# Two roundings of a feed-forward stage: constants formed on ScalarE, and a pair's rounding sum put behind the next pair's scaling

## The reference, cut to what matters

```python
def fp4_quant_dequant(x):            # BLOCK = 16 along the last dimension
    scale = jnp.maximum(jnp.max(jnp.abs(xb), axis=-1, keepdims=True) / 6.0, 1e-12)
    idx = jnp.searchsorted(_MID, jnp.abs(xb / scale))
    return (_GRID[idx] * jnp.sign(xb / scale) * scale).reshape(shape)
...
gate = fp4_linear(x, w_gate)
y = fp4_linear(x, w_up)
h = jax.nn.silu(gate) * y
return fp4_linear(h, w_down)         # both operands of fp4_linear are quantised
...
x = x + 0.5 * _L0_ffn_ref(_layernorm(x, axis=-1), L0_ffn_w_gate, L0_ffn_w_up, L0_ffn_w_down)
```

## Time and profile before

| | us |
|---|---|
| runs of the kernel, median of 3 | 1034.25 (1032.65 to 1035.71) |
| the profiled execution, its own time | 1042.43 |
| its span, first to last instruction | 1040.7 |
| FP4 stage one: first h (L307) to last residual (L315) | 40.94 to 107.09 |
| FP4 stage two: the same | 435.18 to 500.63 |

### The profile page before, as it was taken

How to read it: one execution, slowest core, us unless ns; L and a number is a source line. 1 busy time by engine, 2 the same in 40 slices (tenths; PEclk the granted TensorE clock), 3 DMA queues, 4 the chain that set the end, 5 groups by cost and what they waited for, 6 DMA issues and landing times. The chain is left out here.

```text
span 1040.7 us, 15374 instructions
## 1 busy us (share of the span) xinstructions
PE 739.7 (71%) x5487; PEld 502.4 (48%) x5487; DVE 710.3 (68%) x1213; ACT 346.7 (33%) x591; POOL 414.6 (40%) x597
## 2 busy tenths in 40 slices
PE   0566897777779995476577925488887778467694
PEld 0345455776679984254544613233333333254462
DVE  8997778999958885998342337678887786054132
ACT  0211381110015500122112514066766666411152
POOL 4344304888859601344151532223223332115053
PEclk9987899999969998688587967589999999868797
DMA  8000000000000003100012126484000000001213
GB/s 190 10 1 1 1 1 1 1 1 1 1 1 2 1 1 92 45 1 0 1 37 71 41 76 203 107 125 68 9 7 9 8 8 8 7 0 34 70 37 106
DMA packets 43024, 35.98 MB, mean 35 GB/s; under 512 B 6182, under 2 KB 37478, under 8 KB 42950
## 3 DMA queue, kind: packets, MB, share of 16 engines
q1 hardware_dynamic: 40390, 29.68, 12.2%
q0 software_dynamic: 2560, 5.31, 1.5%
HBM read 17.51 MB, written 15.89 MB: 32 GB/s over the span
## 5 line engine op out<-in xcount | busy, mean ns | idle before, releaser
L1990 DVE TENSOR_REDUCE blockmax<-c_bank 128x8 f32<-128x1024 f32 x144 | 174.9, 1223 | 47.5 <-PE c_bank L2116 41.3
L2053 ACT ACTIVATE PT<-c_bank 128x1024 f32<-128x1024 f32 x144 | 145.4, 1025 | 71.4 <-PE c_bank L2138 71.3
L2152 PE MATMUL c_bank<-PT,V 128*9 128x256 f32 (+3 forms) x960 | 78.6, 431 | 14.5 <-POOL PT L1942 10.4
L897 PE MATMUL sums<-prod,ident 128*128 128x128 f32 x512 | 68.2, 290 | 26.6 <-DVE prod L929 26.6
L2109 PE MATMUL c_bank<-KA,QA 48*128 48x128 bf16 (+3 forms) x608 | 59.9, 282 | 36.1 <-DMA KA<-qk_parts_dram 16.3
L1942 POOL TENSOR_SCALAR_AFFINE_SELECT PT<-PT 128x256 f32<-128x256 f32 x128 | 49.0, 406 | 80.8 <-ACT PT L2053 80.8
L897 PEld LDWEIGHTS sums<-prod,ident 128*128 128x128 f32 x512 | 62.7, 200 | 31.9 <-DVE prod L929 31.7
L1648 POOL DMA_INDIRECT routed_results<-results_m,rows_m x48 | 45.9, 957 | 78.0 <-DVE results_m L1625 74.9
L2138 PE MATMUL c_bank<-QA,KA 51*128 51x128 bf16 (+3 forms) x480 | 56.9, 302 | 16.7 <-DMA QA<-nrows 16.1
L1631 DVE TENSOR_TENSOR r_h_m<-r_silu_m,r_gu_m 128x256 f32<-128x256 f32 x48 | 20.2, 421 | 67.1 <-ACT r_silu_m L1616 67.1
L379 PE MATMUL gu_f<-gu_wT,xqT_f 128*128 128x352 f32 x128 | 52.9, 568 | 16.9 <-DVE h_f L307 16.9
(11 more groups left out here) (337 smaller groups left out, 1818.6 us busy)
## 6 DMA issues: line engine op xcount, KB each, us to landing
sorted_rows<-blank SPq DMA_DIRECT2D x2, 1584.0 KB, 12.2
rows_m<-sorted_rows SPq DMA_DIRECT2D x12, 264.0 KB, 4.4
qk_parts_dram<-qk_parts SPq DMA_DIRECT2D x8, 384.0 KB, 3.4
QA<-qk_parts_dram SPq DMA_DIRECT2D x6, 384.0 KB, 7.4
KA<-qk_parts_dram SPq DMA_DIRECT2D x6, 384.0 KB, 9.2
back_m<-routed_results SPq DMA_DIRECT2D x8, 256.0 KB, 3.8
qk_parts_dram<-qk_parts SPq DMA_DIRECT2D x8, 256.0 KB, 3.4
m_gu<-in_rt_gate SPq DMA_DIRECT2D x1, 1024.0 KB, 5.6
```

Of the source, the lines that this page charges most:

```text
L897: ins = nc.tensor.matmul(sums[:, kind, 0], k.ident[:, :], prod[:, kind, e // HALF, :, e % HALF, :], start=(e == 0), stop=(e == DH - 1))
L1990: nc.vector.tensor_reduce(blockmax[:, h % 2, :, HALFQ * n:HALFQ * (n + 1)], slot_of((1, m)).rearrange("p b (n c) -> p b n c", c=P), AX.X, ...
L2053: nc.scalar.activation(PT[:, u % PRING, :, :], slot_of((0, u)), ACT.Exp, scale=SCALE).then_inc(s_pt, 1)
L2152: ins = nc.tensor.matmul(O[32 * g:32 * g + DH + 1, f * P:f * P + n], V[:, b, j, h, :], PT[:, u % PRING, b, o:o + n], start=(j == 0), stop= ...
```

## The change

Only the quantising of h changes, in both FP4 stages. ACT forms the magic number in two operations on the 128 x 704 tile, Relu(p - 1) and then 1.5 x 2^22 x (p' + 1) as one multiply and add, in place of DVE's one operation L173; bias operands are two new columns, `less` and `more`, filled by DVE at the stage's start. Scaled values go to a new tile `hs` with two slots. On DVE the rounding sum of pair j (now `round_h(j)`) is put behind `quantise_h(j+1)`, which holds the first six steps of the next pair. The condition `wait(dve, s_hq, j - 1)` in `quantise_h(j)` is left as it is.

```diff
+    def on_vector_scaled(self, ch, src, slot, xs, s_power):
...
+        ch.link(nc.vector.tensor_tensor(self.blocks(xs), self.blocks(src), self.spread(self.inv[:, :]), ALU.mult))
+        nc.vector.tensor_scalar(magic.bitcast(I32), xs.bitcast(I32), EXPONENT_BITS, None, ALU.bitwise_and).then_inc(s_power, 1)
+
+    def on_scalar_above(self, slot, less):
+        magic = self.magic[:, slot, :]
+        return self.nc.scalar.activation(magic, magic, ACT.Relu, bias=less)
+
+    def on_scalar_magic(self, slot, more):
+        magic = self.magic[:, slot, :]
+        return self.nc.scalar.activation(magic, magic, ACT.Identity, bias=more, scale=GRID_MAGIC)
+
+    def on_vector_sum(self, slot, xs):
+        return self.nc.vector.scalar_tensor_tensor(self.y[:, slot, :], xs, ONE_BELOW, self.magic[:, slot, :], ALU.mult, ALU.add)
...
+        hs = k.sb(f"hs{tag}", [P, 2, W2], ctx=ctx)
+        less = k.sb(f"less{tag}", [P, 1], ctx=ctx)
+        more = k.sb(f"more{tag}", [P, 1], ctx=ctx)
...
-                    qh.on_vector(chh, h[:, :, :].rearrange("p s c -> p (s c)"), j % 2, s_hy)
+                    qh.on_vector_scaled(chh, h[:, :, :].rearrange("p s c -> p (s c)"), j % 2, hs[:, j % 2, :], s_power)
+
+                def round_h(j):
+                    dve.wait_ge(s_magic, j + 1)
+                    qh.on_vector_sum(j % 2, hs[:, j % 2, :]).then_inc(s_hy, 1)
...
+                quantise_h(0)
                 for j in range(PAIRS):
-                    quantise_h(j)
+                    if j + 1 < PAIRS:
+                        quantise_h(j + 1)
+                    round_h(j)
...
+                def magic(j):
+                    act.wait_ge(s_power, j + 1)
+                    qh.on_scalar_above(j % 2, less[:, 0:1]).then_inc(s_above, 1)
+                    act.wait_ge(s_above, j + 1)
+                    qh.on_scalar_magic(j % 2, more[:, 0:1]).then_inc(s_magic, 1)
...
+                magic(0)
                 for j in range(PAIRS):
                     if j + 2 < PAIRS:
                         gate(j + 2)
+                    if j + 1 < PAIRS:
+                        magic(j + 1)
                     hidden_columns(j)
```

More of the change, by code:

```diff
@@ L161, in spread @@
         return ap.unsqueeze(2).to_broadcast([P, self.nb, QBLOCK])
-    STEPS = 7
+    def on_vector_scaled(self, ch, src, slot, xs, s_power):
+        nc, magic = self.nc, self.magic[:, slot, :]
+        ch.link(nc.vector.tensor_reduce(self.amax[:, :], self.blocks(src), AX.X, ALU.max, apply_absolute_value=True))
+        ch.link(nc.vector.tensor_scalar(self.scale[:, slot, :], self.amax[:, :], 1.0 / 6.0, 1e-12, ALU.mult, ALU.max))
+        ch.link(nc.vector.reciprocal(self.inv[:, :], self.scale[:, slot, :]))
+        ch.link(nc.vector.tensor_tensor(self.blocks(xs), self.blocks(src), self.spread(self.inv[:, :]), ALU.mult))
[8 more added lines that the diff above has]
+        return self.nc.vector.scalar_tensor_tensor(self.y[:, slot, :], xs, ONE_BELOW, self.magic[:, slot, :], ALU.mult, ALU.add)
     def on_vector(self, ch, src, slot, s_y):
@@ L276, in fp4_ffn @@
         qh = Quant(k, f"h{tag}", W2, ctx)
+        hs = k.sb(f"hs{tag}", [P, 2, W2], ctx=ctx)
+        less = k.sb(f"less{tag}", [P, 1], ctx=ctx)
+        more = k.sb(f"more{tag}", [P, 1], ctx=ctx)
+        s_const, s_power, s_above, s_magic = (k.sem(f"{n}{tag}") for n in ("s_const", "s_power", "s_above", "s_magic"))
         gu = k.ps(f"gu{tag}", [P, 2, 2, BANK], ctx=ctx)
@@ L315, in residual @@
                     nc.vector.scalar_tensor_tensor(xs, y[:, j % 2, 0:2 * D], 0.5, xs, ALU.mult, ALU.add).then_inc(s_res, 1)
+                nc.vector.memset(less[:, :], -1.0)
+                nc.vector.memset(more[:, :], GRID_MAGIC).then_inc(s_const, 1)
                 if prepare:
@@ L440, in _ @@
                 gate(1)
+                act.wait_ge(s_const, 1)
+                magic(0)
                 for j in range(PAIRS):
```

## The result

| | us |
|---|---|
| the kernel before, median of 6 runs | 1034.98 (1032.65 to 1038.26) |
| the changed kernel, median of 6 | 1050.86 (1046.85 to 1055.53) |
| ratio of the runs, 95% interval | 1.0151 (1.0114 to 1.0189) |
| profiled execution, own time and span, before | 1042.43, 1040.7 |
| the same, changed | 1051.57, 1049.8 |

What follows compares the result with a forecast made beforehand. DVE set the pace before, at 6.70 us a pair; afterwards two loops would, with a swinging clock, at 8.83. Each stage grows 10.6 us, two stages 21.3, so 1034.25 + 21.3 = 1055.5 us; range 1043 to 1067.

Steps and rivals of the forecast that it cites:

- The gain of L173: DVE time freed by removing L173: 0.56 us per pair, 9.0 us for sixteen, if DVE stayed the bound.
- Loop A: FP4 stages, DVE and POOL: L168 waits for POOL's work behind the rounding sum; period 7.23 us.
- loop B: FP4 stages, all engines, two pairs long through PE's in-order work: 14.71 us, 7.36 per pair; limit at high clock.
- Loop C: One-pair loop through PE and ACT with both new operations; the prediction gave it only at low clock, 11.04 us.
- The start of a stage: First sums of a stage: last input quarter until 64.5, sum of pair 2 ending at 70.0 in stage one.
- The operations on ACT: Relu and Identity on ACT: 0.85 us each, hidden by 0.14 us at the high clock.
- The clock: PE's clock swings, four tenths of the steady part low: 8.83 us per pair, between ends of 7.36 and 11.04.
- the 2.88: PE idle time in us, before the change, behind which slow operations stood; taken as a gap that lost the clock.
- the formula 4P - 24.7: Lengthening of one stage, P being the steady period per pair: 10.6 us at 8.83; two stages 21.3 us.
- The end of a stage: POOL does pairs 6 and 7 back to back, 6.5 us; from POOL's last end to the residual nothing changes.
- the first rival: PE's clock stays high in both stages: 7.36 us per pair, +9.4, 1043.7 us; chance 0.20.
- The idle time of DVE: Profile sign: DVE idle about 2.1 us a pair, ahead of h for silu and of L168 for POOL's hq.

Runs made afterwards that it cites:

- the edit that cut B: Changed kernel with gate_up and silu taken one pair further ahead on PE and ACT; 1050.37 us, ratio 1.0101.
- both edits: Changed kernel with a third slot for POOL's scale and magic, and gate_up and silu one pair further ahead; 1038.25 us, ratio 0.9998.
- filler: Changed kernel with three unused products on the identity put on PE ahead of the transposes for pairs 2 to 5; 1048.53 us, ratio 1.0137.
- the order without ACT: Changed kernel with L173 put back on DVE and no magic number work on ACT; 1063.73 us, ratio 1.0230.

## Why the prediction was right

*The bound before and the loops.* Right. The gain of L173 never came, since DVE stopped being the bound. Taking either loop away alone changed the two stages by less than 3 us; taking both away gave a period of 6.02 against the 6.14 worked out for a DVE-bound kernel. Loop A measured 7.19 for 7.23, loop B 7.34 for 7.36. Loop C was named at the low clock only. Its terms in the prediction come to 7.21 at the high clock, as long as A, and every second period measured 7.24; the edit that cut B cut C with it, so they were not told apart.

*The start of a stage.* Right to 0.4 us in stage one, and there in part by luck. Sum(0) ends at 51.81 (51.83 in the sum), L168(2) starts at 55.13 (55.08), sum(1) ends at 58.99 (59.06), the quarter at 64.40 (64.5), sum(2) at 69.68 (70.0). L169 of pair 3 stood 0.60, so it took 0.4 of the 0.6 that I had added. But the 6.00 us from h(0) to h(1) that I carried over came from a gate_up(1) mostly at the low clock, 4.15 us in the trace of before, and by chance 4.30 in that of the changed kernel. In stage two it took 2.60, and sum(2) ended 27.1 us after the first h and not 28.8 as in stage one. Counting stage one twice put 2 us too much into the start of the second.

*The operations on ACT.* 0.87 and 0.88 for 0.85. I had them hidden by 0.14 us. Measured, they are hidden by less than 0.1 in one ordinary period and tie with the transposes in the next. Where gate_up was slow they stood on the path: the copies at 97.44 start 2.55 us after their transposes, where 0.91 is enough. In stage two, where another gate_up follows, the next silu still came 7.24 us later, so nothing of the lost time was made up. The Trainium skill, page "ScalarE: Activation LUTs", section "Rules for kernel authors", gives add, mul and relu to VectorE because it is faster per element, by up to about three times in bf16. The tiles here are fp32, and in this case that choice would have been the slower one: with the operation on DVE the two stages are 11.2 us longer in the changed order and 7.4 longer with both edits, since DVE's 0.56 us lie on the path. The estimate of 0.89 us by that page's budget agrees with the measured 0.87 and 0.88.

*The clock: the term that was mis-sized.* I took four tenths of the steady part at the low clock, P = 8.83. Measured is (100.66 - 69.68)/4 = 7.75 in stage one and (496.48 - 465.66)/4 = 7.71 in stage two. Against my ends of 7.36 and 11.04 that is one tenth. Three periods in four kept the high clock through gaps of 1.45 to 1.64 us ahead of the transposes and 0.94 behind them; one in each stage lost it, behind a gap of 1.63 in stage one and of 1.45 in stage two, so the length of the gap alone does not say which. That period cost 1.6 to 1.7 us and not 3.7, since only part of it was slow. The rows of before had not told on which side a gap of 1.6 us would fall, and I had placed it too near to the 2.88. The 2.88 was itself read too strongly: the slow product at 97.01 in the earlier trace rows stands behind 0.94 us, and in stage two of before the transposes behind such a gap, at 488.08, took 0.88 us, so that the clock fell only behind them. With the measured P, 7.75 and 7.71, the formula 4P - 24.7 gives 6.3 and 6.1 us, measured 6.7 and 5.7. That the sums agree, 12.4 us, is in part luck, since errors in the start and in the end of the stages partly cancel.

*The end of a stage.* 6.5 us in the sum, 107.53 - 100.66 = 6.87 measured. Sum(7) ran beside POOL, took 1.44 and not 0.88, and held POOL's next operation up, 1.91 for 1.39. I had priced the two in a row without their meeting on the port; it is 0.4 us a stage. From POOL's last end to the residual I had said that nothing changes. It is 6.23 us for 5.93, but by other steps: the transposes start 2.13 us after POOL's end, behind PE's product of pair 6, where before they waited for POOL alone, and the last transposes and product gain 1.8 by a higher clock. In the kernels where that clock stayed low the same stretch takes 7.95 us. So here two errors of about 2 us cancelled.

*The rivals.* In the stages the first rival, the clock staying high, was the nearer one: 9.4 us against my 21.3, with 12.4 measured. In the whole time my 1055.5 is nearer to the 1050.9 than its 1043.7, and that is luck: the median's difference of 15.9 has 3.5 more than the stages, in parts that were not changed and that vary by as much. The idle time of DVE, 2.1 us a pair in the forecast, is 2.13 to 2.31 in the ordinary periods.

*What I looked for in the profile* came, but for the steady clock "clearly under 0.92", which is 0.93, and the wait of L168 for POOL, seen once a stage; in the other turns h came late enough that POOL had ended. The shortest periods, 7.24 us, lie a little under the 7.4 that I named.

## What to carry to other kernels

When a consumer's step is moved behind the producer's next step, look for every wait that was comfortable because the handover lay a period back, and for every engine whose program still has the old distance in it; here three such loops lay between 7.19 and 7.34 us, so that mending one alone showed next to nothing and only both edits together did. Extra work on an idle engine is free only where something covers the round trip: the same two ACT operations gained 0.56 us a pair in one order and made a stage some 17 us longer in the other, a part of it by the clock. And read a stage's own length, cut into start, steady part and end, beside the whole time: here unchanged stages moved by up to 10 us between traces, more than most of the edits to be judged, and what a filler won in the steady part the end of the stage lost again.

## What the runs showed of the hardware

With gaps of 1.45 to 1.64 us ahead of the transposes PE kept 2.4 GHz in three periods of four, in each stage of the changed kernel, and with a filler of 1.46 us in them all eight periods kept it. L169, a TENSOR_SCALAR on 44 columns, takes 0.18 us alone and up to 1.19 beside POOL, as a sum on 704 columns with two SBUF inputs takes 0.88 and, beside POOL, up to 2.25 (the last pair of the order without ACT); in the other direction POOL's 1.39 became 1.91. The Trainium skill, page "SBUF — State Buffer", section "Who interferes with whom", says that DVE and GpSimd share one pair of ports as an exclusive lock, which one of them holds for a whole instruction; the trace agrees. With L169 taken away, the period fell by 0.4 to 0.5 us and DVE's next wait was for silu.
